# Short operations taken off GpSimd, and a part's value products issued behind one burst of scores

## The reference

```python
x = x + squared(layernorm(x))     # q, k normalised per head; weights (q.k)^2, causal; divided by their sum; @ Wo.T
x = x + gated(layernorm(x))       # one k and v per token, picked by a top-1 gate; softmax per head
x = x + mqa(layernorm(x))         # one k and v for all heads (with biases); softmax per head; @ out_w.T + out_b
x = x + gated(layernorm(x))
# layernorm(x) = (x - mean) / sqrt(var + 1e-5) over the 512 channels
```

## Time and profile before

| | before |
|---|---|
| median of 3 runs | 4744.71 us (4744.14 to 4746.26) |
| profiled execution, its own time | 4741.89 us |
| its span | 4740.1 us |
| mean granted TensorE clock | 0.918 of full |
| busy: PE, POOL, DVE, ACT | 81%, 63%, 40%, 34% |

### The profile page before, as it was taken

How to read it: one execution, slowest core, us unless ns; L and a number is a source line. 1 busy time by engine, 2 the same in 40 slices (tenths; PEclk the granted TensorE clock), 3 DMA queues, 4 the chain that set the end, 5 groups by cost and what they waited for, 6 DMA issues and landing times. The chain is left out here.

```text
span 4740.1 us, 66857 instructions
## 1 busy us (share of the span) xinstructions
PE 3849.7 (81%) x26018; PEld 1585.2 (33%) x26018; DVE 1899.4 (40%) x4874; ACT 1630.1 (34%) x2433; POOL 2991.2 (63%) x2215
## 2 busy tenths in 40 slices
PE   6788888985978688688786888888798886977975
PEld 4343434322333233233232333333333332323332
DVE  1212212222544444444444445444544444544452
ACT  1543444551223223323333333333233233232333
POOL 2967777983254646547676676776557466465587
PEclk9899998987989889899898999999899997988998
DMA  1001010003000100100101010010001001010010
GB/s 62 18 1 37 18 36 19 19 19 103 18 1 1 54 1 8 48 1 21 34 17 38 1 34 21 23 32 25 30 1 54 1 19 36 1 53 2 1 37 27
DMA packets 63382, 115.05 MB, mean 24 GB/s; under 512 B 8672, under 2 KB 9184, under 8 KB 63072
## 3 DMA queue, kind: packets, MB, share of 16 engines
q1 hardware_dynamic: 63072, 110.77, 7.2%
HBM read 77.19 MB, written 33.55 MB: 23 GB/s over the span
## 5 line engine op out<-in xcount | busy, mean ns | idle before, releaser
L775 ACT ACTIVATE probs_soft<-banks 128x1024 f32<-128x1024 f32 (+1 forms) x960 | 848.6, 936 | 1426.0 <-PE banks L1078 1411.1
L688 POOL TENSOR_TENSOR added_soft<-added_soft,probs_soft 128x2048 f32<-128x2048 f32 (+3 forms) x384 | 1163.9, 3031 | 67.0 <-ACT probs_soft L775 47.9
L867 DVE CUSTOM_DVE_ANT_0 banks<-banks,mask 128x128 f32<-128x128 f32 (+3 forms) x1536 | 700.7, 525 | 739.1 <-PE banks L1093 739.1
L862 DVE TENSOR_REDUCE maxima_soft<-banks 128x2 f32<-128x1024 f32 x384 | 452.4, 1221 | 527.1 <-PE banks L1093 527.1
L1093 PE MATMUL banks<-k_soft,q_soft 32*128 32x512 f32 (+3 forms) x4608 | 531.4, 555 | 140.4 <-ACT probs_soft L775 140.3
L781 ACT ACTIVATE probs_squared<-banks,key_scale_squared 128x512 f32<-128x512 f32 (+3 forms) x768 | 379.2, 590 | 382.5 <-PE banks L1078 371.6
L665 POOL TENSOR_SCALAR_AFFINE_SELECT probs_soft<-probs_soft 128x512 f32<-128x512 f32 x384 | 239.7, 637 | 427.7 <-ACT probs_soft L775 427.6
L1078 PE MATMUL banks<-q_soft,k_soft 32*128 32x512 f32 (+3 forms) x4608 | 505.7, 521 | 0.0
L1131 PE MATMUL banks<-probs_soft,v_soft 128*32 128x512 f32 (+3 forms) x4608 | 454.2, 514 | 46.0 <-POOL probs_soft L665 31.7
L688 POOL TENSOR_TENSOR added_squared<-added_squared,probs_squared 128x2048 f32<-128x2048 f32 (+3 forms) x128 | 390.2, 3048 | 7.3 <-ACT probs_squared L781 1.9
L1075 PE MATMUL banks<-shift_soft,ones 32*128 32x512 bf16 (+3 forms) x2304 | 205.4, 344 | 227.2 <-DVE maxima_soft L867 136.4
(11 more groups left out here) (153 smaller groups left out, 4801.0 us busy)
## 6 DMA issues: line engine op xcount, KB each, us to landing
tiles_soft<-out SPq DMA_DIRECT2D x96, 256.0 KB, 2.9
rest_soft<-out SPq DMA_DIRECT2D x96, 256.0 KB, 3.0
out<-rest_soft SPq DMA_DIRECT2D x96, 256.0 KB, 2.1
tiles_squared<-in_x SPq DMA_DIRECT2D x32, 256.0 KB, 2.9
rest_squared<-in_x SPq DMA_DIRECT2D x32, 256.0 KB, 3.2
out<-rest_squared SPq DMA_DIRECT2D x32, 256.0 KB, 2.0
raw_wq<-in_squared_wq SPq DMA_DIRECT2D x1, 1024.0 KB, 5.6
raw_wk<-in_squared_wk SPq DMA_DIRECT2D x1, 1024.0 KB, 7.9
```

Source lines behind the costliest of these rows:

```text
L688: ins = pool.tensor_tensor(sums, sums, slot(ph, n)[:, :, col:col + width], ALU.add)
L775: ins = act.activation(slot(ph, n)[:, 2 * a:2 * a + 2, 0:width], score_pair(e, a)[:, :, 0:width], ACT.Exp, scale=SCALE)
L862: ins = dve.reduce_max(m["maxima"][:, ph % 2, 2 * a:2 * a + 2, t, p], score_pair(e, a)[:, :, col:col + width], AX_X)
L867: ins = dve.tensor_tensor_reduce(scores, scores, k["mask"][:, CHUNK - width:CHUNK], 1.0, MASKED, ALU.add, ALU.max, m["maxima"][:, ph % 2, ...
```

## The change

1. **Normalising.** In the second act nothing is computed from the loaded tile. Mean and variance are taken by DVE when the tile is written (`ostat`, right behind `out`, for the stages whose result is normalised later), POOL computes 1/sqrt and shift for a whole stage in two operations on 8 columns (`oscale`), and the normalising itself becomes one ACT operation (`norm`, Identity with scale and bias), placed two tiles ahead of its `ln`. In the first act DVE still takes the moments of the loaded tile and POOL 1/sqrt and the shift of each tile; ACT normalises.
2. **Squares** (`ksq`, `qsq`) go from POOL to ACT.
3. **Split of maxima** (`mxr`) goes from POOL to DVE, five operations of 128x16 behind DVE's own reduction.
4. **Value products**: `av` leaves `HALVED`, and `phase` no longer places its first half: all products of a part stand at the half behind.
5. A residual tile is reloaded only after its moments are taken (`rload` behind `ostat`).

```diff
-HALVED = ("av", "q", "q2", "k2", "v2", "ks", "kall", "vall")
+HALVED = ("q", "q2", "k2", "v2", "ks", "kall", "vall")
...
+def norm_events(kind, s):
+    lead = [("stats", s, t) for t in range(NT)] if kind == "squared" else []
+    events = lead[:3] + [("norm", s, t) for t in range(2)]
     for t in range(NT):
+        events += lead[t + 3:t + 4]
+        if t + 2 < NT:
+            events.append(("norm", s, t + 2))
         events.append(("ln", s, t))
         if t + TILES < NT:
             events.append(("load", s, t + TILES))
     return events
+
+
+def out_events(kinds, s):
+    kept = kinds[s] == "squared" or s + B < len(kinds)
+    events = [("rload", s, t) for t in range(TILES)]
+    for t in range(NT + 1):
+        if t < NT:
+            events.append(("out", s, t))
+        if t:
+            if kept:
+                events.append(("ostat", s, t - 1))
+            if t - 1 + TILES < NT:
+                events.append(("rload", s, t - 1 + TILES))
+    return events + [("oscale", s)] * kept
...
         h = VALUES_AT[part]
-        at[h].append(("more", ("av", of, part)))
         at[h + 1].append(("av", of, part))
...
 (ACT)
+                elif u == "norm":
+                    act.wait_ge(sg.tile_in[t % TILES], DMA * (2 * s + t // TILES + 1))
+                    if not soft:
+                        act.wait_ge(sg.scales_in, place["stats", s, t] + 1)
+                    elif s >= B:
+                        act.wait_ge(sg.scales_out, s - B + 1)
+                    x = m["tiles"][:, t % TILES, :]
+                    act.activation(x, x, ACT.Identity, scale=k["rstd"][:, b, t:t + 1], bias=k["shift"][:, b, t:t + 1])\
+                        .then_inc(sg.normed, 1)
+                elif u == "ksq":
+                    act.activation(m["key_square"][:, c], k_of(ph)[:, CHUNK * c:CHUNK * c + CHUNK], ACT.Square)\
+                        .then_inc(sg.key_squares, 1)
...
 (DVE)
+                elif u == "ostat":
+                    if kind_of(s) == "gated":
+                        dve.wait_ge(sg.summed, earlier("out", ("out", s, t), "gated") + 1)
+                    else:
+                        wait_free(dve, ("out", s, t))
+                    moments(m["rest"][:, t % TILES, :], stages[s][1], t).then_inc(sg.out_variance, 1)
+                    dve.wait_ge(sg.out_variance, place[e] + 1)
...
 (SP)
+                    last = ("ostat", s, t - TILES) if t >= TILES else ("ostat", s - 1, t + TILES)
+                    if last in place:
+                        sp.wait_ge(sg.out_variance, place[last] + 1)
                     sp.dma_start(m["rest"][:, t % TILES, :], rows_of(source, s, t)).then_inc(sg.rest_in[t % TILES], DMA)
```

More of the change, by code:

```diff
@@ L239, in plan @@
     first, rest = keys_and_values(kinds[0], 0)
-    events = [("load", 0, t) for t in range(TILES)] + norm_events(0) + first
+    events = [("load", 0, t) for t in range(TILES)] + norm_events(kinds[0], 0) + first
     if soft:
@@ L253, in plan @@
         halves = [h for g in range(NG) for h in phase(kinds, NG * s + g)]
[L254 to L257, removed]
+        outs = out_events(kinds, s - 1) if s else []
         half = next((n for n, e in enumerate(outs) if e == ("out", s - 1, TPC)), 0)
@@ L267, in plan @@
             first, rest = keys_and_values(kinds[s + 1], s + 1)
-            work.append(([("load", s + 1, t) for t in range(TILES)] + norm_events(s + 1), 0, NG * HALVES))
+            work.append(([("load", s + 1, t) for t in range(TILES)] + norm_events(kinds[s + 1], s + 1), 0, NG * HALVES))
             work.append((first + rest, 2 * HALVES + 5, NG * HALVES))
@@ L272, in plan @@
     events += [("add", last, NKB - 1), ("av", last, "C"), ("sm", last, 1)] + [e for e, _ in sums_done(kinds[-1], last, 1)]
-    events += [("rload", stages - 1, t) for t in range(TILES)]
-    for t in range(NT):
-        events += [("out", stages - 1, t)] + [("rload", stages - 1, t + TILES)] * (t + TILES < NT)
+    events += out_events(kinds, stages - 1)
     return two_banks(events)
@@ L535, in act_program @@
     order = {name: [e for e in events if e[0] == name] for name in
-             ("load", "rload", "stats", "out", "mxr", "krep", "vst", "ksq", "qsq", "kvar", "nrm", "rs", "rw", "gate")}
+             ("load", "rload", "stats", "norm", "out", "ostat", "mxr", "krep", "vst", "ksq", "qsq", "kvar", "nrm", "rs", "rw", "gate")}
     order["picks"] = [e for e in events if e[0] in ("kall", "vall")]
@@ L834, in then, with moments @@
                 dve.wait_ge(sg.vector_step, steps.next())
+            def moments(x, b, t):
+                then(dve.bn_stats(k["stats"][:], x))
+                then(dve.bn_aggr(k["mean_var"][:], k["stats"][:]))
+                dve.tensor_scalar(k["minus_mean"][:, b, t:t + 1], k["mean_var"][:, 0:1], -1.0, None, ALU.mult)
+                return dve.tensor_scalar(k["var_eps"][:, b, t:t + 1], k["mean_var"][:, 1:2], EPS, None, ALU.add)
+            if soft:
+                for c in range(NC):
+                    dve.memset(m["shift_cols"][:, c].rearrange("p t i d -> p (t i d)"), 0.0).then_inc(sg.cleared, 1)
+                dve.wait_ge(sg.cleared, NC)
             def each(x):
@@ L880, in _ @@
                     dve.wait_ge(sg.tile_in[t % TILES], DMA * (2 * s + t // TILES + 1))
[L881 to L888 removed]
+                    moments(m["tiles"][:, t % TILES, :], stages[s][1], t).then_inc(sg.variance, 1)
+                    dve.wait_ge(sg.variance, place[e] + 1)
+                elif u == "ostat":
+                    _, s, t = e
+                    if kind_of(s) == "gated":
+                        dve.wait_ge(sg.summed, earlier("out", ("out", s, t), "gated") + 1)
+                    else:
+                        wait_free(dve, ("out", s, t))
+                    if not soft:
+                        dve.wait_ge(sg.scales_in, NT * (s + 1))
+                    elif s >= B:
+                        dve.wait_ge(sg.scales_out, s - B + 1)
+                    moments(m["rest"][:, t % TILES, :], stages[s][1], t).then_inc(sg.out_variance, 1)
+                    dve.wait_ge(sg.out_variance, place[e] + 1)
                 elif u == "gtt":
```

106 lines of the change are left out of this document (46 added, 60 removed).

## The result

| | before | after |
|---|---|---|
| median | 4744.43 us of 4 runs (4742.96 to 4746.26) | 5076.53 us of 4 runs (5071.47 to 5085.87) |
| ratio | | 1.0702, interval 1.0683 to 1.0721 |
| profiled execution, span, mean granted clock | 4741.89, 4740.1, 0.918 | 5085.87, 5083.9, 0.889 |

What follows compares the result with a forecast made beforehand. PE, busy 3849.7 of 4740.1 us, was taken as the bound, through its waits and clock. Terms -100 - 27 - 35 - 25 + 84 + 40 - 15 + 10 = -68 gave 4674, forecast 4677 us, range 4600 to 4785.

Steps and rivals of the forecast that it cites:

- the split: Split of maxima moved to DVE: five operations near 185 ns, about 1.3 us a time, covered; -25 us (0 to -32).
- Boundaries: Starts of new stages in the second act: PE's transposes wait less once ACT normalises; -100 us (0 to 171 gained).
- squares: Key squares on ACT, no longer queued behind POOL's adds: PE waits less; -27 us (bounds -10 and -45).
- moments: Moments at a gated stage's output: DVE's ostat waits for POOL's add, PE behind it; +10 us (bound 228).
- clock: PE's granted clock: +40 us for dips at added short gaps (0 to 77); -15 for fewer long boundary waits.
- rival 4: DVE stands at the output moments, waiting for POOL's adds, over 60 us idle as sign; 4767 us, chance 0.07.
- rival 5: ACT stands for tile landings ahead of normalising, sign over 100 us with PE waiting behind; 4777 us, chance 0.08.
- Value products: Whole value products at one half leave added empty gaps between PE's bursts; +84 us (0 to 112).
- masks: PE's value products wait less for POOL's masks, as av stands a burst later; -35 us (0 to -50).
- Rival 3: Added empty gaps between bursts, with clock dips, outweigh gains; about 4780 us, 4796 at worst; clock below 0.90; chance 0.12.

## Why the prediction was wrong

**The step that failed** is the split: "On DVE five operations near 185 ns with a wait for completion each, about 1.3 us a time", covered by the `keys` burst, of which nothing was charged and from which 25 us were to come back. It took the price of an operation that reads one SBUF tensor and reduces, and gave it to casts and to subtractions of two SBUF tensors. They measured 5.6 us a time, 8.4 in the one shown above, because most of them stood for a running POOL operation, and a `keys` burst does not cover that: PE stood 160.9 us ahead of `mxt`. With operations that really take near 0.2 us the term came out: 27 us below the split on POOL with value products in halves (4595.38 against 4622.04, on one chip), where -25 was forecast. With whole ones it is 11 us (4693.67 against 4704.53, on two chips), which these runs do not tell from nothing. In its place stands +372. The bound of that step, 125 us, was no bound, because it was made of the same 1.3 us.

**Without that term the sum holds.** Leaving out the -25, the forecast for the change without its split was 4702. The run of it has a ratio of 0.9923, which is 4708 on the 4744.43 of before.

**Boundaries, squares, moments.** -100, -27, +10 and -15 for the clock make -132; measured -120 together. Squares alone were -43 where -27 was charged, so the normalising with its moments and the clock gives about -77 (120 - 43) where -105 was charged. The tiles' transposes wait 101.2 us, as forecast. DVE's wait for them ahead of its moments is 6.0 us in 64 (rival 4 is out), as the second row says at its end; the first is ACT's normalising:

```profile
L785 ACT ACTIVATE tiles_soft<-tiles_soft,norm_shift,rstd 128x512 f32<-128x512 f32 x96 | 77.1, 814 | 139.7 <-DMA tiles_soft<-out 139.5
...
L855 DVE BATCH_NORM_STATS2 stats<-rest_soft 128x6 f32<-128x512 f32 x64 | 43.7, 683 | 6.2 <-POOL rest_soft L737 6.0
```

ACT does stand 139.5 us for landings, beyond the 100 that I had named as rival 5's sign. The gain of 120 us came all the same, so most of that idle time is not on the path. It was a bad sign by itself: PE's own wait, 101.2, is the one to read.

**Value products, masks, clock.** +84, +40 and -35 make +89; measured +79 alone (4815.66 - 4736.95), 82 with the split on POOL (4704.53 - 4622.04), 98 with reductions (4693.67 - 4595.38). Beside the slow split it is 160 (5076.53 - 4916.92). The parts do not add: 293 and 79 alone with the 120 of the rest make 252, and the change is 332. The missing 80 us lie between these two parts, since the split costs 293 or 295 us beside halves (the latter 4916.92 - 4622.04) and 372 beside whole products. In the traces PE's waits for the split's last cast go from 102.3 us with halves to 124.7 with whole products, and those for L891's maxima from 108.8 to 146.5; where the remainder comes from is not shown.

**Rival 3** had named a clock below 0.90 as its sign, and the sign came: 0.889. Its mechanism did not: what the gaps cost stayed near the forecast. In the profiled executions the mean clock followed PE's idle time, whatever had made it: 867 us at 0.923 (the change without its split), 944 at 0.908 (whole value products alone), 1093 at 0.899 (the split alone), 1139 at 0.889 (the change). So this sign could not tell rival 3 from another loss. One of its sums was wrong too: with the dip in one gap of two, 81 x (1.4 + 0.8) = 178 us, and the time would be 4731 and not 4780. The Trainium skill, TensorE: Matmul & The Clock Gate, "A second HAM failure mode: psum-queue depth-cycling", says that brief idling of PE between groups of matmuls, if frequent, makes the clock go back and forth between its levels. The run with whole value products alone agrees in direction: 0.908 to 0.917 in its four runs, where the kernel before has 0.913 to 0.919 beside it.

## What to carry to other kernels

Before a short operation is moved to VectorE beside long GpSimd operations, look for rows of its own kind there: same source memory, same number of SBUF inputs. If its mean is several times its shortest, and the long ones end where a GpSimd operation ends, it is standing for GpSimd, and of five dependent ones each can stand again. A minimum, median and maximum of the line shows it at once, where a mean of another operation on the same size shows nothing. Where the work must be on VectorE, a form with one input that only reduces (here over an axis of one) did the same for 0.2 us, and turned a loss of 7% into a gain of 1%, and with the value products in halves of 3.2%.

## What the runs showed of the hardware

- A VectorE cast of 128x16 in SBUF takes 202 ns at best and 3572 at worst beside GpSimd's adds of up to 4.5 us; a reduction of the same size takes 186 ns on the mean beside the same adds (93 of 96 began while GpSimd was in an operation, none took over 190 ns), and moments of 128x512 take 683. With the adds cut short the three casts take 227, 203 and 274 ns.
- An operation that stood ended at a fixed distance behind the GpSimd operation: a cast of 128x16 55 to 64 ns behind its end, a subtraction of the same size 34 to 44, a multiplication of 128x512 with both inputs in SBUF 541 to 553.
- Two VectorE operations on 128x512 in the changed kernel, each with two inputs, one of them in PSUM in the one case and both in SBUF in the other, take 692 ns and 1504 on the mean. The first takes 691 to 693 ns each time. The second takes 691 at the shortest, 693 in the median and 4980 at the longest: the 15 of 32 that began while GpSimd was in an operation took 2.43 us on the mean, the other 17 took 0.69.

```profile
L1004 DVE TENSOR_TENSOR y_squared<-y_squared,sums_squared 128x512 f32<-128x512 f32 x32 | 48.1, 1504 | 1.1
...
L996 DVE TENSOR_TENSOR y_squared<-banks,y_squared 128x512 f32<-128x512 f32 x16 | 11.1, 692 | 169.5 <-PE banks L1174 169.5
```

- An ACT Identity with scale and bias on 128x512 from SBUF to SBUF takes 814 ns, above both rows that bounded it, 688 from PSUM and POOL's 768.
